# Scores of a 16-head attention from pairs of 64-row tiles with keys masked to one head of four, and ScalarE's copy of the transposed rows moved up

## Time and profile before

| what | value |
|---|---|
| median of 3 runs | 558.21 us (556.32 to 561.12) |
| profiled execution | 557.38 us, span 555.6 us |
| busy share of the span | PE 90%, PEld 75%, ACT 48%, DVE 42%, POOL 36% |
| attention steps 0 to 15 | 25.43 to about 237 us of the span |
| first expert tile | 248.56 us |
| one ordinary step (step 9) | 144.76 to 157.38 us |

### The profile page before, as it was taken

One profiled execution on the slowest core, in us unless ns is written; L12 is line 12 of the kernel. 1 busy time (PEld: TensorE's weight loads), 2 busy tenths in 40 slices (PEclk: granted clock), 3 DMA queues, 4 the chain that ended last, 5 costly groups with the idle time before them and its releaser, 6 DMA issues.

```text
span 555.6 us, 13098 instructions
## 1 busy us (share of the span) xinstructions
PE 501.0 (90%) x3742; PEld 418.6 (75%) x3743; DVE 233.6 (42%) x1083; ACT 264.9 (48%) x1003; POOL 200.3 (36%) x186
## 2 busy tenths in 40 slices
PE   4889889999999989949999999999999999999980
PEld 2557656666666666629999999999999999999970
DVE  2677787787788777831232111111111111111110
ACT  1267688777877777853432233333323323333310
POOL 3031233334544554411325553333333333333321
PEclk9899999999999999998999999999999999999996
DMA  8890030203030313644656665666666666666615
GB/s 265 249 343 11 21 96 21 95 21 97 20 103 25 103 28 102 203 158 117 182 178 191 188 186 146 180 172 186 179 185 185 191 188 183 173 173 170 166 19 160
DMA packets 51005, 78.61 MB, mean 141 GB/s; under 512 B 10529, under 2 KB 39473, under 8 KB 50769
## 3 DMA queue, kind: packets, MB, share of 16 engines
q1 hardware_dynamic: 40160, 66.80, 37.2%
q0 software_dynamic: 8592, 10.58, 11.4%
q10 hardware_dynamic: 2208, 0.71, 0.6%
HBM read 68.27 MB, written 11.90 MB: 144 GB/s over the span
## 4 chain that ended last, share of the span: by engine, by line
PE 53%; issue 26%; POOL 9%; DMA 5%; DVE 2%; ACT 2%; POOLq 0%; DVEq 0%; SPq 0%; ACTq 0%
PE psVO L958 22%; PE psS L946 12%; PE psP L946 12%; POOL kbd L263 3%; DMA fold<-xn_dram,sel 3%; POOL meta_dram L441 3%; ACT prob L588 2%; POOL rstd L430 2%; PE psQK L934 2%; PE psQK L784 1%; DMA meta_dram<-meta,pos 1%; PE psP L817 1%; PE psVO L838 1%; DMA sum_dram<-fold,sel 1%; PE psVO L795 1%
## 5 line engine op out<-in xcount | busy, mean ns | idle before, releaser
L958 PE MATMUL psVO<-xw,prob 128*128 x624 | 141.7, 380 | 0.8 <-DVE fold L1349 0.8
L958 PEld LDWEIGHTS psVO<-xw,prob 128*128 128x128 f32 x624 | 115.5, 190 | 15.7 <-issue 1.2
L487 POOL DMA_INDIRECT sum_dram<-fold,sel x39 | 62.0, 1590 | 163.0 <-DMA sel<-meta_dram 103.0
L588 ACT ACTIVATE prob<-prob,smin 128x128 f32<-128x128 f32 x256 | 99.5, 395 | 16.7 <-DVE smin L1124 16.7
L674 ACT ACTIVATE prob<-psS,b1T 128x128 f32<-128x128 f32 x160 | 45.6, 368 | 96.8 <-PE psS L946 96.8
L674 ACT ACTIVATE prob<-psP,b1T 128x128 f32<-128x128 f32 x152 | 43.3, 368 | 92.2 <-PE psP L946 87.5
L430 POOL TENSOR_TENSOR rstd<-ve,minus_half 128x1 f32<-128x1 f32 x32 | 33.1, 1033 | 142.8 <-DVE ve L1087 136.9
L946 PEld LDWEIGHTS psS<-fold,w1c 128*128 128x128 f32 x640 | 76.8, 197 | 1.9 <-DVE fold L1344 1.0
L946 PE MATMUL psS<-fold,w1c 128*128 128x128 f32 x640 | 77.3, 280 | 0.6 <-DVE fold L1344 0.6
L946 PEld LDWEIGHTS psP<-fold,w1c 128*128 128x128 f32 x608 | 70.8, 192 | 0.9
L946 PE MATMUL psP<-fold,w1c 128*128 128x128 f32 x608 | 71.0, 275 | 0.0
(11 more groups left out here) (165 smaller groups left out, 533.0 us busy)
## 6 DMA issues: line engine op xcount, KB each, us to landing
w1c<-in_L_ffn_W SPq DMA_DIRECT2D x39, 1024.0 KB
xw<-in_x SPq DMA_DIRECT2D x16, 512.0 KB, 7.5
xw<-in_L_ffn_W SPq DMA_DIRECT2D x8, 1024.0 KB, 6.2
sum_dram<-h_all SPq DMA_DIRECT2D x17, 128.0 KB
xn_dram<-xn SPq DMA_DIRECT2D x16, 128.0 KB
out<-sum_dram SPq DMA_DIRECT2D x4, 512.0 KB, 5.5
relb<-in_L_ffn_b SPq DMA_DIRECT2D x1, 1024.0 KB, 5.5
sel<-meta_dram SPq DMA_DIRECT2D x39, 2.0 KB
```

What stands on the lines that cost most here:

```text
L487: pool.indirect_dma_start(out=sum_dram.ap()[0:EARLY_B * S if j < EARLY else N_TOK + P, :], out_offset=bass.IndirectOffsetOnAxis(ap=row_no[ ...
L588: i = act.activation(blk, blk, ACT.Exp, bias=smin[:, k:k + 1], scale=-1.0, accum_out=ssum[:, k:k + 1])
L958: i = pe.matmul(psVO[:, 0:D], hT[u][:, c * P:(c + 1) * P], xw2[:, bass.ds(e * (HC * D) + c * D, D)], start=(c == 0), stop=(c == HC - 1))
```

## The change

- `scores(b, w)` replaces `scores(b, c)`: two matmuls, one over rows 0 to 63 (heads 0 to 3 of the chunk) into psS0 and one over rows 64 to 127 (heads 4 to 7) into psS1, each against 512 columns. It waits until both buffers are empty. Two calls in a step in place of four.
- The keys are masked to one head in four instead of one in eight: kbd is 128 x 512 for each chunk. The mask pmask is made once by DVE.
- `values(b, w)` takes the eight heads of a chunk in one call and waits for both pT buffers; `biased` c waits for the pair of matmuls.
- Heads are in natural order, so `spread` is one copy instead of two, and the bias table is loaded in order.
- PE's order: `turn_xn2` and `turn_x(i+1)` come before the second `values` and the second `scores`.
- ACT's order: `x1T_evac(i+1)` before `exp(i, 1)`; `first_group` runs one image further ahead, in the middle of the step, before `exp(i, 0)`.

```diff
@@ mask_keys
             if later(b):
                 eng.wait_ge(s_ps, NCH * b)
+            else:
+                eng.wait_ge(dv_const, 3)
             eng.tensor_tensor(
-                chunks(kbd[:, c * HPC * S:(c + 1) * HPC * S], HPC, S),
-                under(qkT[:, (DC + c) * S:(DC + c + 1) * S], HPC), over(hmask[:, :], S), ALU.mult) \
+                chunks(kbd[:, c * CH * S:(c + 1) * CH * S], CH, S),
+                under(qkT[:, (DC + c) * S:(DC + c + 1) * S], CH), over(pmask[:, :], S), ALU.mult) \
                 .then_inc(k_sb[c], 1)
@@ ScalarE
-            def step(i, u, front=True, back=True, late=True, nxt=True, batch=None, tanh=False):
-                if nxt:
-                    first_group(i + 1)
+            def step(i, u, front=True, back=True, late=True, nxt=True, batch=None, tanh=False, ahead=True):
                 if back:
                     exp(i - 1, 1 - u, 2)
...
                     r_evac(i - 1)
+                if ahead:
+                    first_group(i + 2)
                 if front:
                     exp(i, u, 0)
                 if late:
                     x2T_evac(i - 2)
-                if front:
-                    exp(i, u, 1)
                 if nxt:
                     x1T_evac(i + 1)
                 if front:
+                    exp(i, u, 1)
                     v_evac(i)
...
+            first_group(1)
             step(0, 0, back=False, late=False)
             step(1, 1, late=False)
-            step(2, 0, tanh=True)
+            step(2, 0, tanh=True, ahead=False)
             select_exps(1, NG, B)
+            first_group(NG)
@@ TensorE
-            def scores(b, c):
-                if c % 2 == 0:
-                    pe.wait_ge(k_sb[c // 2], b + 1)
-                if isinstance(b, int) and b == 0 and c < 2:
+            def scores(b, w):
+                pe.wait_ge(k_sb[w], b + 1)
+                if isinstance(b, int) and b == 0 and w == 0:
                     pe.wait_ge(rel_sb, 5)
                 else:
-                    pe.wait_ge(s_min, NCH * b + c - 1)
-                w = c // (NCH // DC)
-                pe.matmul(psS[c % 2][:, :], qkT[:, w * S:(w + 1) * S], kbd[:, c * CH * S:(c + 1) * CH * S],
-                          start=True, stop=True).then_inc(s_ps, 1)
+                    pe.wait_ge(s_min, NCH * b + 2 * w)
+                for r in range(2):
+                    rows = slice(r * HALF, (r + 1) * HALF)
+                    pe.matmul(psS[r][:, :], qkT[rows, w * S:(w + 1) * S], kbd[rows, w * CH * S:(w + 1) * CH * S],
+                              start=True, stop=True).then_inc(s_ps, 1)
...
-            def values(b, c):
-                if c == 0:
+            def values(b, w):
+                if w == 0:
...
-                pe.wait_ge(pT_sb, NCH * b + c + 1)
-                for n in range(CH):
-                    i = pe.matmul(psCX[n * PART:(n + 1) * PART, c // 2 * S:(c // 2 + 1) * S],
-                                  v_s[:, v_at(c, n):v_at(c, n) + PART],
-                                  pT[c % 2][:, n * S:(n + 1) * S], start=(c % 2 == 0), stop=(c % 2 == 1))
-                i.then_inc(pv_ps, 1)
+                pe.wait_ge(pT_sb, NCH * b + 2 * w + 2)
+                for j in range(2):
+                    for n in range(CH):
+                        k = 2 * n + j
+                        i = pe.matmul(psCX[n * PART:(n + 1) * PART, w * S:(w + 1) * S],
+                                      v_s[:, v_at(w * HPC + k):v_at(w * HPC + k) + PART],
+                                      pT[k // CH][:, k % CH * S:(k % CH + 1) * S], start=(j == 0), stop=(j == 1))
+                i.then_inc(pv_ps, 2)
@@ TensorE, step
                 if back:
                     values(i - 1, 0)
-                    values(i - 1, 1)
                     context(i - 1, 1 - u, 2)
                 if front:
                     scores(i, 0)
                 if back:
                     context(i - 1, 1 - u, 3)
                     spread_sums(i - 1)
+                if late:
+                    turn_xn2(i - 2, batch)
+                if nxt:
+                    turn_x(i + 1)
+                if back:
+                    values(i - 1, 1)
                 if front:
                     scores(i, 1)
-                if back:
-                    values(i - 1, 2)
-                    values(i - 1, 3)
-                if late:
-                    turn_xn2(i - 2, batch)
-                if front:
-                    scores(i, 2)
-                if nxt:
-                    turn_x(i + 1)
-                if front:
-                    scores(i, 3)
                 if late:
                     gate_logits(i - 2)
@@ VectorE
+            dve.tensor_reduce(pmask[:, :], hmask[:, :].rearrange("p (f m) -> p m f", f=2), AX.X, ALU.add) \
+                .then_inc(dv_const, 1)
...
             def biased(b, u, c):
-                dve.wait_ge(s_ps, NCH * b + c + 1)
+                dve.wait_ge(s_ps, NCH * b + c // 2 * 2 + 2)
...
-                for c in range(DC):
-                    i = dve.tensor_copy(srcw[:, c * P:(c + 1) * P].rearrange("p (n j d) -> p n j d", n=CH, j=2),
-                                        srcp[:, c * HPC:(c + 1) * HPC].rearrange("p (j n) -> p n j", n=CH).unsqueeze(3)
-                                        .to_broadcast([P, CH, 2, HD]))
+                i = dve.tensor_copy(chunks(srcw[:, :], HEADS, HD), over(srcp[:, :], HD))
```

More of the change, by code:

```diff
@@ L28 @@
 CH = 4
+HALF = 64
 NCH = HEADS // CH
@@ L105, in vit_layer_kernel @@
         hmask = sb("hmask", [P, HPC])
+        pmask = sb("pmask", [P, CH])
         tb1 = sb("tb1", [P, 1])
@@ L271, in own_wait, with v_at @@
             eng.sem_inc(waited[eng.engine], 1)
-        def v_at(c, n):
-            return (c // 2 * HPC + 2 * n) * PART + c % 2 * HD
+        def v_at(h):
+            return h // 2 * 2 * PART + h % 2 * HD
         def part(t, a, b):
@@ L283, in load_mirror @@
             eng.dma_start(chunks(rel_mirror[:, c * CH * S:(c + 1) * CH * S], CH, S),
-                          bass.AP(rel_dram, (c // 2 * HPC + c % 2) * (NREL + 1),
-                                  [(1, P), (2 * (NREL + 1), CH), (1, S)])).then_inc(rel_in, 16)
+                          bass.AP(rel_dram, c * CH * (NREL + 1),
+                                  [(1, P), (NREL + 1, CH), (1, S)])).then_inc(rel_in, 16)
         block = ctx.enter_context(nc.Block())
@@ L400, in _ @@
             pool.affine_select(out=hmask[:, :], in_=hmask[:, :], compare_op=ALU.is_ge, fill=0.0,
-                               base=0, pattern=[[-HD, 2], [-2 * HD, CH]], channel_multiplier=1) \
+                               base=0, pattern=[[-HD, HPC]], channel_multiplier=1) \
                 .then_inc(gp_const, 1)
@@ L418, in _ @@
             pool.affine_select(out=hmask[:, :], in_=hmask[:, :], compare_op=ALU.is_ge, fill=0.0,
-                               base=HD - 1, pattern=[[HD, 2], [2 * HD, CH]], channel_multiplier=-1) \
+                               base=HD - 1, pattern=[[HD, HPC]], channel_multiplier=-1) \
                 .then_inc(gp_const, 1)
@@ L650, in _ @@
             x1T_evac(0)
+            first_group(1)
             step(0, 0, back=False, late=False)
             step(1, 1, late=False)
-            step(2, 0, tanh=True)
+            step(2, 0, tanh=True, ahead=False)
             select_exps(1, NG, B)
+            first_group(NG)
             gated = {first + n + 2: g for g, (first, n) in enumerate(BATCHES[:-1])}
             for i in range(3, B - 1):
-                step(i, i % 2, batch=gated.get(i))
-            step(B - 1, 1, nxt=False, batch=gated.get(B - 1))
-            step(B, 0, front=False, nxt=False)
+                step(i, i % 2, batch=gated.get(i), ahead=i + 2 < B)
+            step(B - 1, 1, nxt=False, batch=gated.get(B - 1), ahead=False)
+            step(B, 0, front=False, nxt=False, ahead=False)
             act.wait_ge(pv_ps, NCH * B)
```

## The result

| | before | after |
|---|---|---|
| median (4 runs each) | 557.82 us (556.32 to 561.12) | 537.95 us (536.94 to 540.05) |
| profiled execution, span | 557.38 us, 555.6 us | 538.68 us, 536.9 us |
| ratio of times | | 0.9641, 95% interval 0.9587 to 0.9695 |

The change makes the kernel 20 us faster. Two more comparisons, each with its own runs of the kernel before, gave 0.9672 (0.9638 to 0.9706) and 0.9663 (0.9627 to 0.97).

What follows compares the result with a forecast made beforehand. A loop of waits, with no engine full, was taken to set the attention steps. From 557.38 us, 18.4 (11 steps of 1.67) and 5.9 (steps 0 to 3) came off: 533.1, forecast 533 us, range 525 to 549.

Steps and rivals of the forecast that it cites:

- the likeliest case: Whole kernel: all parts of the change work as summed, 533 us, own range 527 to 539; chance 57%.
- x1T's order: End of each step: x1T before exp(i, 1) brings the next project_qk about 0.8 after x2T, gain 1.4 us a step.
- The pair: Scores on TensorE: two 64-row tiles overlap, 0.95 us a pair; TensorE's work falls from 11.55 to about 9.9.
- A: Rival for the scores: the tiles do not overlap, a pair is 1.72, the kernel 547 us; chance 16%.
- rival B: Rival whose claim the given text leaves out; counted among the faster outcomes, chance 12%.
- Masks and both buffers: Each step: masks about 0.62 (VectorE) and 0.95 us (POOL), biased(i, 0) at +7.53; waits for both buffers hidden.
- rival C: Handing over both buffers, and VectorE behind it, give the gain back: loop grows 1.5 us, 554 us; chance 8%.
- The loop: Ordinary step: waits through VectorE, biased(i, 0), exp(i, 0), x2T and gate_logits set its length, 12.62 to 10.95 us.
- Steps 4 to 14: Eleven attention steps: each 1.67 us shorter, gate and rank steps given the same gain, 18.4 us in all.
- Steps 0 to 3: First steps: about 1.5 us in step 0, 0.9 each in 1 and 2, 2.6 in step 3; sum 5.9.
- rival D: Slower: row tiles cost more than the whole-array matmul, or the clock halves; 2.6 us a pair, 570 us; chance 5%.
- Behind the steps: Step 15 to the first expert tile, and the expert stretch: both keep their length, no change.

Runs made afterwards that it cites:

- experiment 3: The kernel before with only ScalarE's new order (x1T before exp(i, 1), first_group one image ahead): 545.97 us, ratio 0.9789.
- experiment 5: The kernel after with x1T back behind exp(i, 1) and four unused matmuls behind gate_logits: 552.99 us, ratio 0.9896.
- experiment 2: The kernel after with each scores matmul over all 128 rows instead of 64: 554.53 us, ratio 0.9933.
- the repeat: The kernel after, unchanged, run and profiled again: 538.66 us, ratio 0.9672.
- experiment 9: The kernel after with the first image sums moved into step 0, behind project_v: 538.26 us, ratio 0.9673.
- experiment 8: The kernel after with seven unused matmuls in TensorE's wait at the end of step 2: 537.19 us, ratio 0.9657.
- experiment 4: The kernel after with x1T back behind exp(i, 1), first_group left where it is: 564.94 us, ratio 1.009.
- experiment 10: The kernel after with up to four of POOL's record DMAs in flight instead of two: 539.9 us, ratio 0.9689.

## Why the prediction was right, and where it was not

It gave 533 us, range 525 to 549, and 0.87 for faster; the likeliest case's own range was 527 to 539. The time was 537.95. Against the profiled execution the sum forecast 24.3 us and 18.7 came.

**x1T's order: right.** The wait for x1T is gone; x2T to the next project_qk is 0.88 us (143.99 to 144.87), forecast 0.8. Experiments 3 and 5 carry it: undone at full clock it costs 1.24 us a step, forecast 1.4, and ScalarE's new order alone gave 12 us in all.

**The pair: the overlap right, its price low.** 0.95 was taken; it is 1.06, and 1.21 with the 0.09 that it adds to context 2 and the 0.06 to context 3, against 1.72 without overlap (experiment 2). The 0.95 is 0.86 and 0.10; inside the pair the form costs 0.20, since from the first records to the second, and from those to the next instruction, it takes 0.53 each, where a full matmul takes 0.43. TensorE's work in a step came to 10.48 us; the terms of my sum give 10.0 (11.55 less 3.44 plus 1.90), not the 9.9 that I wrote.

A was wrong: the pair took 1.06 us, not 1.72. The first records of both tiles start within 0.01 us of each other and then both second ones, 0.53 later (139.54 and 140.07); in the kernel before, four heads of values put their first records together and then their second ones in the same way (149.35 and 149.48). No run shows a ground for rival B, at 12% in the sum of the chances; what they show is this order of the records, and 0.35 us over a full matmul's 0.86 for a pair with what it adds around it.

**Masks and both buffers: right.** The masks take 0.69 and (GpSimd) 1.03 us, forecast 0.62 and 0.95; biased(i, 0) starts at +7.36, forecast +7.53, and VectorE waits no more on h_all. The second pair starts at +9.46, forecast +9.4, with no marked wait, so rival C, the handing over of the buffers, did not come.

**The loop: named wrong.** I had it through VectorE, biased(i, 0) and exp(i, 0), with first_group covered by 0.25. The last pT copy was forecast at +7.15 and began at +7.61: context 3 starts 0.39 later in the step than before (140.60 less 133.69, against 151.28 less 144.76), 0.20 of it from the pair, 0.08 from context 2 and 0.10 from values, which starts 0.10 later now that it takes both pT copies. Context 3 then takes 0.07 longer to its copy (0.70 from 140.60 to 141.30, 0.63 before), and that makes the 0.46. So rT and first_group ended late and exp(i, 0) began at +8.76, not +8.59, though biased 0 was early. These 0.17 us and 0.05 in gate_logits are nearly all of the 0.23 by which the step is longer than 10.95. VectorE, expected to wait 0.8, waits 1.27.

**Steps 4 to 14: right by a cancellation.** 11 times 1.67 gave 18.4. The ordinary ones (5, 8, 9, 12) gained 1.42 to 1.44, step 4 1.71, the six with gate or rank work, which I had given the same 1.67, gained 1.69 to 2.26 (step 13 went from 13.61 to 11.35). The sum came to 18.8.

**Steps 0 to 3: the step that failed.** Forecast 5.9; 1.1 in the first profile, 2.8 in the repeat (26.11 to 77.25 against 53.92). The masks did what they should: in step 0 biased began 1.37 us earlier (5.13 after the step's start in the repeat, 6.50 before), forecast 1.5; VectorE's first norm, begun 0.13 behind GpSimd's mask, took 1.05 us beside a mask of 1.03 (30.26 to 31.31), where it had taken 1.90 beside one of 1.89. But I let rival D's mechanism, the clock, stand at 5% because it "stood at 1.00 through 145 us with 1 us idle in each step". That row said nothing of a TensorE with less work, nor of a longer wait, and the change brought both. In step 0 the fall goes with the lighter scores: with full rows the image sums took 1.95, behind a single wait of 2.11 us (experiment 2), with row tiles 3.29, behind 1.48; lighter scores alone don't bring it, since it stayed away in experiment 9, where the sums run ahead of that wait. Ahead of step 3 it goes with the wait, which grew because TensorE's part of step 2 became 1.4 us shorter (12.40 to 11.03) and the way to the selection logits only 0.7 (13.31 to 12.63): project_qk took 2.03 behind 0.91 (the kernel before, experiment 3), 3.45 to 3.66 behind 1.59, and 3.52 behind 1.75 even with full rows. Experiment 8, with that wait filled, agrees. In step 0 this is read from profiles side by side; no run changes its work alone. The price: 1.3 us in the image sums (3.29 against 1.96) and some 0.3 in the scores ahead of them, 0.6 at step 3 (experiment 8). With these back steps 0 to 3 would have gained about 5.0 in the repeat. What remains is in steps 1 and 2, 0.4 and 0.7 for 0.9 each. In the first profile step 0 lost another 1.7: it began 2.55 us earlier than in the repeat and ended only 0.86 earlier (36.99 against 37.85).

**Rival D: its mechanism came, not its cost.** Had the change come without x1T's move it would have been slower than the kernel before (experiment 4, 1.009), by just this clock and not by dear row tiles. The move of x1T did not only save its own wait, it kept the clock up (1.00 from 76.39 to 202.97); the parts are worth more together (19.4 us) than one by one (12.0 for ScalarE's order and -6.9 for all but x1T's move, experiments 3 and 4; first_group's move stands in both). D's 2.6 us a pair lies halfway between 1.72 and twice that, serial matmuls at half clock; no run shows a pair that dear. Where the clock was 0.50, at the end of step 0, it took 2.01 us (31.83 to 33.84).

**Behind the steps: unforced.** Step 15 to the first tile and the expert stretch were forecast at no change and cost 3.1 us in the first profile. The repeat has 24.19 for the first, 0.4 above before, and 307.9 for the second; in the other profiles, whose expert stretch is the same, the second lasted up to 310.4 (experiment 10). For the kernel before I have one profile, so how much of either is the change's stays open.

## What to carry to other kernels

Before taking work off an engine whose granted clock can fall, as TensorE's did here behind waits of 1.20 and 1.59 us, look at the waits that will be left beside the smaller work: they may have been harmless only because the work was there, or they may grow because the engine now arrives earlier, and the edit that removes the wait belongs in the same change. Price a 64-row pair by one measured full matmul plus what the form costs inside, ahead and behind (here 0.35 us), not by the ideal, and read the cover of each hidden wait on every path that reaches it: here it failed by the path through TensorE and ScalarE, not by the one through VectorE that had been traced. When a stretch in the middle gets shorter, expect parts of it back at the next DMA whose landing nothing in the change moves (here 3 us earlier at step 15, 1.65 at the first tile, experiment 9).

## What the runs showed that I had not expected

- Two float32 matmuls of 64 rows and 512 columns on the two row halves of the array take 1.06 us together; two of 128 rows 1.72 (experiment 2). The first records of both start together (139.54), then the second ones (140.07).
- With nearly the same wait in each step, 1.07 to 1.19 us in the kernel before and 1.20 in experiment 4, the granted clock stayed at 1.00 in the first and was 0.50 to 0.65 behind seven of eleven in the second. 0.86 us of unused matmuls in each wait made that kernel 11 to 12 us faster (experiment 5).
- Time saved at full clock in front of a queue of another engine is partly paid back: 1.6 us on TensorE at step 3 gave 0.6 (experiment 8).
